# Kernel study: the router's statistics and high parts of all even tiles moved among the heads of a contraction

## The reference, cut to what matters

```python
x = x + _L0_xattn_ref(ctx, ctx, _layernorm(x), ssm_kernel, D, 8)      # long convolution, 32 heads
x = x + _L0_ffn_ref(_layernorm(x), router_w, router_b, expert_w, expert_b)
x = x + _L1_xattn_ref(_layernorm(x), ctx, ctx, Wh, wg_w, wo_w, ...)
x = x + _L1_ffn_ref(_layernorm(x), Wg, Wu, Wd, Wr, Ag, Bg, Au, Bu, Ad, Bd)
...
def _L0_ffn_ref(x, router_w, router_b, expert_w, expert_b):
    logits = xf @ router_w + router_b           # 2048 tokens, 512 features, 16 experts
    S = softmax(logits)
    G, idx = top_k(S.T, 128)                    # each expert picks its 128 best tokens
    out = einsum('ekh,hd->ekd', xf[idx], expert_w) + expert_b
    y = zeros(...).at[idx].add(G[..., None] * out)
```

## Time and profile before

| | |
|---|---|
| median of 3 runs | 1077.47 us (1075.81 to 1080.92) |
| the profiled execution | 1082.89 us |
| its span, first to last instruction | 1080.9 us |
| PE busy | 1045.9 us, 97% of the span |
| DVE, ACT, POOL busy | 580.8, 446.9, 614.0 us |
| last sum of the contraction ends | 188.53 us from the span's start |
| logits complete, softmax starts | 225.31 us |

### The profile page before, as it was taken

One profiled execution on the slowest core, in us unless ns is written; L12 is line 12 of the kernel. 1 busy time (PEld: TensorE's weight loads), 2 busy tenths in 40 slices (PEclk: granted clock), 3 DMA queues, 4 the chain that ended last, 5 costly groups with the idle time before them and its releaser, 6 DMA issues.

```text
span 1080.9 us, 13184 instructions
## 1 busy us (share of the span) xinstructions
PE 1045.9 (97%) x4865; PEld 847.1 (78%) x4865; DVE 580.8 (54%) x1039; ACT 446.9 (41%) x796; POOL 614.0 (57%) x456
## 2 busy tenths in 40 slices
PE   5999998899999999999999999999999999999998
PEld 4777776666689988877788888888888888888886
DVE  6998998848865644784522533325333253342224
ACT  4665444721575547554333322233232233222232
POOL 4888887110224562212367776667766677767662
PEclk9999999889999999999999999999999999999999
DMA  7611210000020020033232222542225332232211
GB/s 242 223 49 62 55 51 20 1 1 1 0 79 1 1 70 1 1 131 138 86 110 74 73 73 73 183 151 98 73 73 170 125 133 76 74 112 93 86 61 39
DMA packets 24543, 85.48 MB, mean 79 GB/s; under 512 B 3152, under 2 KB 4832, under 8 KB 23712
## 3 DMA queue, kind: packets, MB, share of 16 engines
q1 hardware_dynamic: 22432, 81.24, 22.0%
q10 hardware_dynamic: 2048, 3.41, 0.9%
HBM read 74.86 MB, written 9.78 MB: 78 GB/s over the span
## 4 chain that ended last, share of the span: by engine, by line
PE 63%; DVE 1%; POOL 1%; issue 1%; ACT 0%; POOLq 0%
PE banks L318 21%; PE banks L319 20%; PE banks L320 20%; PE banks L313 1%; PE banks L1458 1%; PE banks L1467 0%; POOL wgl L661 0%; DVE stat L1724 0%; POOL gul L687 0%; DVE xres L2112 0%; POOL xtr L644 0%; PE banks L1524 0%; DVE hf L2123 0%; DVE xres L1990 0%; DVE xf L1999 0%
## 5 line engine op out<-in xcount | busy, mean ns | idle before, releaser
L2123 DVE TENSOR_TENSOR hf<-banks,silu 128x512 f32<-128x512 f32 x132 | 91.3, 691 | 323.3 <-PE banks L320 322.1
L687 POOL TENSOR_TENSOR gul<-wst,guh 128x1280 fp32r<-128x1280 f32 x44 | 129.9, 2953 | 142.5 <-DVE guh L2006 135.5
L697 POOL TENSOR_TENSOR hl<-hf,hh 128x512 fp32r<-128x512 f32 x129 | 178.7, 1420 | 8.6 <-ACT hh L1077 8.6
L1113 PE MATMUL banks<-kv,strip 128*128 128x288 f32 x640 | 160.6, 410 | 2.1 <-DVE strip L1656 2.1
L1077 ACT ACTIVATE hh<-hf 128x512 fp32r<-128x512 f32 x132 | 83.6, 633 | 190.3 <-DVE hf L2123 190.3
L1113 PEld LDWEIGHTS banks<-kv,strip 128*128 128x128 f32 x640 | 121.4, 192 | 34.7 <-DVE strip L1656 2.5
L1075 ACT ACTIVATE silu<-banks 128x512 f32<-128x512 f32 x132 | 78.9, 598 | 167.2 <-PE banks L320 167.0
L318 PE MATMUL banks<-xf,guh 128*128 128x512 f32 x352 | 137.2, 390 | 0.9 <-POOL gul L687 0.9
L319 PE MATMUL banks<-xf,guh 128*128 128x512 f32 x352 | 137.0, 389 | 0.0
L320 PE MATMUL banks<-xf,gul 128*128 128x512 f32 x352 | 136.9, 389 | 0.0
L586 POOL TENSOR_TENSOR rstd<-vare,mhalf 128x2 f32<-128x2 f32 x32 | 25.6, 800 | 160.3 <-DVE vare L1737 160.2
(11 more groups left out here) (291 smaller groups left out, 2215.1 us busy)
## 6 DMA issues: line engine op xcount, KB each, us to landing
wst<-in_chunk_w SPq DMA_DIRECT2D x44, 960.0 KB, 4.7
strip<-toep SPq DMA_DIRECT2D x29, 256.0 KB, 3.1
xf_s<-xf SPq DMA_DIRECT2D x2, 2048.0 KB, 6.9
out<-xres SPq DMA_DIRECT2D x16, 256.0 KB, 2.1
xf<-xf_s SPq DMA_DIRECT2D x8, 512.0 KB, 5.8
mk<-hot_s SPq DMA_DIRECT2D x14, 256.0 KB
xres<-in_x ACTq DMA_DIRECT2D x4, 512.0 KB, 7.9
xres<-in_x SPq DMA_DIRECT2D x2, 1024.0 KB, 5.4
```

Source lines behind the costliest of these rows:

```text
L687: pool.tensor_tensor(gul[:, u, :], wst[:, u, 0:GU_W], f(guh[:, u, :]), ALU.subtract).then_inc(gul_ready, 1)
L697: pool.tensor_tensor(hl[:, u, s, :], hf[:, s, :], f(hh[:, u, s, :]), ALU.subtract)\
L1113: mm = pe.matmul(dst, strip[:, h % 3, far:far + P], view(kv, h % 3, m * BATCH * PAIRS, [[PAIRS, BATCH], [1, PAIRS]]), start=m == 0, stop=m ...
L2123: dve.tensor_tensor(hf[:, s, :], banks[:, 7, :], silu[:, s % 2, :], ALU.mult).then_inc(mul_done, 1)
```

## The change

`LOG_ORDER` becomes all even tiles, then all odd tiles. Four pairs instead of two (`CONV_PAIRS`) have their statistics taken among the heads, one tile a head, in heads 23 to 30 instead of 24 to 27; POOL's first two roots stand at heads PAIR_HEAD + 3 and + 5, so they come a head earlier, and the two others behind its last head; pairs 2 and 3 use new small buffers (`slots`). ACT makes `high(0)` to `high(3)` and `apply(2)` ahead of END_CONV. The tail of the router is written anew on PE, ACT and DVE: one pair of odd tiles a turn, `LOW_ACT` gains i = 6, the expert part is taken between pairs 2 and 3, and each group of logits is one block.

```diff
-        LOG_ORDER = (0, 2, 4, 6, 1, 3, 5, 7, 8, 10, 9, 11, 12, 14, 13, 15)
+        LOG_ORDER = tuple(range(0, TILES, 2)) + tuple(range(1, TILES, 2))
-        SUM_HEAD, PAIR_HEAD = HEADS // 2 + 2, HEADS // 2 + 8
-        LOW_ACT = (0, 2, 4, 8, 12)
-        CONV_PAIRS = 2
+        SUM_HEAD, PAIR_HEAD = HEADS // 2 + 2, HEADS // 2 + 7
+        LOW_ACT = (0, 2, 4, 6, 8, 12)
+        CONV_PAIRS = 4
...
+            pair_root(2)
+            pair_root(3)
+            pool.wait_ge(pair_rstd, CONV_PAIRS)
...
+            act.wait_ge(y_free, HEADS - 1)
+            act.wait_ge(pr_pool, HEADS - 1)
+            for i in range(4):
+                high(i)
+            apply(2)
             after(act, END_CONV)
-            for n in range(TILES // 2):
-                if n > 1:
-                    apply(n)
-                if n == 6:
+            low(0)
+            low(2)
+            for n in range(3, TILES // 2):
+                apply(n)
+                if n == 7:
                     logits_out(0)
-                if n > 0:
-                    low(2 * n - 2)
-                high(2 * n)
-                high(2 * n + 1)
+                high(2 * n - 2)
+                high(2 * n - 1)
+                low(2 * n - 2)
+            high(TILES - 2)
+            high(TILES - 1)
...
-            for i in range(4):
-                turn_x(i)
+            turn_x(0)
+            turn_x(1)
+            leave_low(0)
+            turn_x(2)
+            turn_x(3)
+            leave_low(2)
             after(pe, END_CONV)
-            turn_o(4)
-            turn_o(5)
-            leave_low(0)
+            turn_o(8)
+            turn_o(9)
+            turn_x(4)
+            turn_x(5)
             pe.wait_ge(pick_set, 3)
             pe.wait_ge(wB_ready, 2 + KB)
...
+            for n in range(3, TILES // 2):
+                if n < TILES // 2 - 1:
+                    for i in (2 * n + 4, 2 * n + 5):
+                        if i < TILES:
+                            summed(pe, i - 2)
+                            turn_o(i)
+                if n == 3:
+                    expert_parts(KB)
+                leave_low(2 * n - 2)
+                turn_x(2 * n)
+                turn_x(2 * n + 1)
+                if n == 6:
                     low_made(pe, 1)
+                    low_made(pe, 9)
+                    for k in range(KB):
+                        logits(0, k)
                 if n == 7:
+                    low_made(pe, 11)
+                    for k in range(KB):
+                        logits(1, k)
                     by_token(0)
...
-                if PAIR_HEAD <= h < PAIR_HEAD + 4:
+                if PAIR_HEAD <= h < PAIR_HEAD + EVENS:
                     n, j = divmod(h - PAIR_HEAD, 2)
                     pair(n, (j,))
             after(dve, END_CONV)
...
-            low(TILES - 4)
-            low(TILES - 3)
-            low(TILES - 2)
-            low(TILES - 1)
+            low(1)
+            for n in range(CONV_PAIRS, TILES // 2):
+                add_conv(2 * n)
+                add_conv(2 * n + 1)
+                pair(n)
+                for i in ((3,), (5, 7), (9, 10), (11, 13))[n - CONV_PAIRS]:
+                    if n < TILES // 2 - 1:
+                        low(i)
+            low(11)
+            low(13)
+            low(14)
+            low(15)
```

More of the change, by code:

```diff
@@ L142, in build, with slots @@
             ("ebx", [P, DIM], F32R), ("pick", [P, P], F32R), ("minus", [P, P], F32R), ("bitc", [P, 3 * STEPS + 1], I32), ("whf", [P, RHEADS, P], F32))
+        stat62, mom2, vare2, rstd2, nmr2 = place(
+            W_AT + 20480, ("stat62", [P, GROUP, 6], F32), ("mom2", [P, GROUP, 2], F32), ("vare2", [P, 2, GROUP], F32),
+            ("rstd2", [P, GROUP], F32), ("nmr2", [P, GROUP], F32))
+        def slots(n):
+            s = slice(2 * (n % 2), 2 * (n % 2) + 2)
+            if n in (2, 3):
+                return stat62[:, s, :], mom2[:, s, :], vare2[:, :, s], rstd2[:, s], nmr2[:, s]
+            return stat6[:, s, :], mom[:, s, :], vare[:, :, s], rstd[:, s], nmr[:, s]
         ye, = place(XH_AT, ("ye", [P, KB * TOKENS], F32))
@@ L579, in pair_root @@
             def pair_root(n):
-                s = slice(2 * (n % 2), 2 * (n % 2) + 2)
+                _, means, var, roots, negated = slots(n)
                 if n < CONV_PAIRS:
                     pool.wait_ge(pair_stats, 2 * n + 2)
-                    pool.tensor_scalar(vare[:, 0, s], mom[:, s, 1], EPS, None, ALU.add).then_inc(pair_var, 1)
+                    pool.tensor_scalar(var[:, 0, :], means[:, :, 1], EPS, None, ALU.add).then_inc(pair_var, 1)
                 pool.wait_ge(pair_var, n + 1)
-                pool.tensor_tensor(rstd[:, s], vare[:, 0, s], mhalf[:, s], ALU.pow).then_inc(pair_pow, 1)
+                pool.tensor_tensor(roots, var[:, 0, :], mhalf[:, 0:2], ALU.pow).then_inc(pair_pow, 1)
                 pool.wait_ge(pair_pow, n + 1)
                 if n < CONV_PAIRS:
-                    for j in range(s.start, s.stop):
-                        i = pool.tensor_scalar(nmr[:, j:j + 1], mom[:, j, 0:1], rstd[:, j:j + 1], -1.0, ALU.mult, ALU.mult)
+                    for j in range(2):
+                        i = pool.tensor_scalar(negated[:, j:j + 1], means[:, j, 0:1], roots[:, j:j + 1], -1.0,
+                                               ALU.mult, ALU.mult)
                     i.then_inc(pair_rstd, 1)
                 else:
-                    pool.tensor_tensor(nmr[:, s], vare[:, 1, s], rstd[:, s], ALU.mult).then_inc(pair_rstd, 1)
+                    pool.tensor_tensor(negated, var[:, 1, :], roots, ALU.mult).then_inc(pair_rstd, 1)
             root(0)
@@ L628, in low @@
                                    by_eighth(f(cch[:, q % 2, :])), ALU.subtract).then_inc(ccl_ready, 1)
-            for n in range(2, TILES // 2):
+            for n in range(CONV_PAIRS, TILES // 2):
                 pair_root(n)
@@ L773, in apply @@
                     rows = ret if 2 * TILES <= i < 3 * TILES else xres
-                    act.activation(xn[:, j, :], rows[:, tile_of(i), :], ACT.Identity,
-                                   bias=nmr[:, j:j + 1], scale=rstd[:, j:j + 1]).then_inc(xn_ready, 1)
+                    _, _, _, roots, negated = slots(n)
+                    act.activation(xn[:, i % GROUP, :], rows[:, tile_of(i), :], ACT.Identity,
+                                   bias=negated[:, i % 2:i % 2 + 1], scale=roots[:, i % 2:i % 2 + 1]).then_inc(xn_ready, 1)
             for i in range(4):
@@ L1710, in pair @@
             def pair(n, part=range(2)):
-                s = 2 * (n % 2)
-                if n >= 2:
+                stats_of, means, var, _, _ = slots(n)
+                if n == 2:
+                    dve.wait_ge(wB_ready, 1 + KB)
+                if n in (CONV_PAIRS, CONV_PAIRS + 1):
+                    dve.wait_ge(pair_rstd, CONV_PAIRS)
+                    dve.wait_ge(xn_ready, 2 * n - 6)
+                elif n > CONV_PAIRS:
                     dve.wait_ge(xn_ready, 2 * n - 2)
@@ L1723, in pair @@
                     tile = LOG_ORDER[2 * n + j] if n < TILES // 2 else (2 * n + j) % TILES
-                    i = dve.bn_stats(stat6[:, s + j, :], rows[:, tile, :])
+                    i = dve.bn_stats(stats_of[:, j, :], rows[:, tile, :])
                 if 1 not in part:
@@ L1729, in pair @@
                 for j in range(2):
-                    i = dve.bn_aggr(mom[:, s + j, :], stat6[:, s + j, :])
+                    i = dve.bn_aggr(means[:, j, :], stats_of[:, j, :])
                 i.then_inc(pair_stats, 1)
@@ L1758, in _ @@
             after(dve, END_CONV)
-            for n in range(1, TILES // 2):
-                if n > 1:
-                    pair(n)
-                if n in (1, 2, 4, 6):
-                    for i in SUM_ORDER[TILES // 2 + (0, 2, 4, 6)[(1, 2, 4, 6).index(n)]:][:2]:
-                        add_conv(i)
-                if n > 1:
-                    low(2 * n - 4)
-                    low(2 * n - 3)
-            low(TILES - 4)
-            low(TILES - 3)
-            low(TILES - 2)
-            low(TILES - 1)
+            low(1)
+            for n in range(CONV_PAIRS, TILES // 2):
+                add_conv(2 * n)
[8 more added lines that the diff above has]
+            low(15)
             n_vec = [0]
```

29 lines of the change are left out of this document (5 added, 24 removed).

## The result

The changed kernel took 1081.6 us (median of 7 runs, 1080.8 to 1084.0), the kernel before, run beside it, 1076.4 (1075.4 to 1080.9). The ratio is 1.0045, 95% interval 1.003 to 1.0059: 4.8 us slower, under the 0.5% at which I put a difference that can be told, and 4.4 was forecast. The two profiled executions don't show it in their spans: 1080.9 us before, 1080.2 changed.

The account below looks back on a forecast made before the run. PE, busy 97% of the span, bounds the kernel, so the seam only shifts what follows. Terms 0.8 + 0.1 + 1.0 + 1.4 = 3.3, plus 1.1 for the clock: 1077.47 + 4.4 = 1081.9 us, range 1077 to 1087.

Parts of the forecast that it names:

- Contraction's end, +0.8: Heads 23 to 30: POOL's roots delay sums and heads 28 to 30 lose catch-up room; last sum ends 0.8 us later.
- the roots' hits: POOL's pair roots, 1.59 us each, at heads 26 and 28 make DVE's sums of heads 27 and 29 wait.
- To the last pair, +0.1: Contraction's end to last pair: 3.5 us of pairs and 2 us of high parts removed return as waits; 20.0 against 19.9.
- Both stalls: Between contraction's end and last pair: ACT stands 4.1 us at low(4), DVE idles 2.6 us ahead of low(10).
- high(12), +1.0: Router tail: ACT makes high(12) only after logits_out(0), so turn_x(15) comes 6.8 behind the last pair's start instead of 5.9.
- logits(1) as one block, +1.4: Router tail on PE: all four blocks of logits(1) follow the last turn instead of one; six more matmuls of 0.24.
- The clock, +1.1 taken from 0 to 2.3: PE's wait from 210.7 to 214.8 may drop its clock to half, making the tail late; total +3.3 if it stays, +5.6 if not.
- The point between: Total of +4.4 us, chosen between +3.3 (PE's clock stays full) and +5.6 (it falls).
- Slower by over 0.5%, the clock decides: Rival, PE between 203 and 220: half clock costs middle 1 and tail 2.3, total +6.6, 1084; chance 0.35.
- The other losses: Middle of the seam: turns at half clock lengthen each round of turn, high, low by 0.4, so the middle loses 1.
- The stalls do not bind: Rival: ACT not held at low(4), DVE not at low(10); softmax -3.1 us, 1074.4; 0.15 with the third rival.
- the third rival: Nothing moves: the search's half-clock stretch starts elsewhere, returning 2 to 3 us; +2, 1079.5; 0.15 with the stalls rival.

Follow-up runs that it names:

- the last kernel: Changed kernel with all winning edits together (pairs a head earlier, expert part, low(10) and logits_out(0) later, high(12) earlier), against the kernel before: ratios 0.9996 and 0.9986.

## Why the prediction was right

**The time.** 1081.9 forecast, 1081.6 measured. That these two agree within 0.3 us is partly luck: the forecast added 4.4 to a median of three runs (1077.47), and with seven the kernel before has 1076.42, which is 5.2 below the changed one. What can be compared is the sum of +4.4 against +4.9 in the seam (two profiles of each) and +4.8 by the ratio.

**Contraction's end, +0.8.** Measured +0.85 (D1, both pairs of profiles). The waits stand where they were forecast, at the sums of heads 27 and 29. I named two causes together, the roots' hits and the bn_stats behind them. The run with the pairs a head earlier has the same hits and D1 as before: the hits cost nothing that lasts once head 30 is free of bn_stats, and with bn_stats there DVE has no room to catch up. Putting the roots a head later only moved the hit. No run has bn_stats at head 30 without the hits, so whether it would cost anything alone stays open.

**To the last pair, +0.1.** Measured 19.72 and 19.40, against 19.87 and 19.12 before: -0.15 by the first pair of profiles, +0.28 by the second, both within what two profiles of one kernel differ by. Both stalls are where the text put them: ACT 3.86 us at low(4) (forecast 4.1), DVE 2.52 at low(10) (2.6). That they, and not the work, set this stretch is shown: either one taken away brought the last pair 2.9 us nearer, both together (with the pairs a head earlier) 5.2 to 6.0.

**high(12), +1.0, and logits(1) as one block, +1.4.** With the clock held, the run with matmuls in the gap has logits(1) 7.10 behind the last pair instead of 6.25, +0.85, and from there to the softmax 12.03 instead of 10.66, +1.37. Both terms hold within 0.2, by this one profile.

**The clock, +1.1 taken from 0 to 2.3.** This was the mis-sized term of the sum: 2.15 in the first profile (21.28 against 19.13), 1.26 in the second (20.39 against the same 19.13), on average 1.7. The point between was a guess between ends. It rested on a reading that does not hold: the text says that rows show the clock at both levels "after waits of this length", that is some 4 us, but the waits ahead of its two rows were shorter, 2.36 and 1.31 us ahead of 189 and 1.01 ahead of 211:

```profile
186.20 1.06 PE L1165 MATMUL banks<-cst,xn 128*128 128x128 f32 x8 [2.36 <-DVE pr L1697]
...
210.97 0.63 PE L1165 MATMUL banks<-cst,xn 128*128 128x128 f32 x4 [1.01 <-DVE xtl L1743]
```

So the full clock at 211 was no evidence that the clock would stay through 3.9. In the four profiles with the gap as in the changed kernel (2.34 us in the second one, 3.9 in the three others) it fell to half every time, in the gap or right behind it. The text also took 4 us as the longest half-clock stretch; it was 6.8 us in the first profile, of which 1.2 lay in the gap.

By the Trainium skill (TensorE: Matmul & The Clock Gate, section The HAM clock gate) the throttled state is the default one and idle time brings it back, and by that rule alone the sum was +5.6. The window at 209, idle and granted 0.66, agrees with it, and the first profile's seam (+5.07) lies between the two sums.

**The rivals.** "Slower by over 0.5%, the clock decides" was close: the clock fell in its place, between 203 and 220, at a price of 1.3 to 2.2 us where it needed 2.1. The other losses it needed (turns at half clock in the middle) did not come in the first profile, and the two ratios, 1.0045 and 1.0051, lie on both sides of its 0.5%. "The stalls do not bind" is refuted by the two edits that took them away. The search was 1.8 us shorter in one profile of the changed kernel and as long as before in the other: the third rival's effect exists, but two executions of one kernel differ by it, so it is not shown to come from the change.

## What to carry to other kernels

When work is taken off two engines that hand tiles to each other in program order, first look for the instruction in each that stands behind a third engine's long block: here 5.5 us of work removed were given back to within 0.3 us by two such places, and moving one block (the expert part) took back some 3.4 of the 4.8 us lost. A filler belongs where its engine would otherwise stand and nothing that follows is ready yet, not merely "somewhere early" or in front of the last step that others wait for: the same block cost 2.9 us ahead of leave_low(4) and gained 1.3 to 2.2 in the gap ahead of leave_low(12). And a gap on PE can be priced twice: once by its length if it is on the path, once by what runs at half clock behind it, here 1.3 to 2.2 us.

## What was not expected of the hardware

The granted clock is no function of the program alone. The same kernel kept 1.00 from 190 to 220 in one execution and fell to 0.50 at 202.3 in another, in the middle of back-to-back matmuls, some 1 to 3 us behind short gaps (1.06 us, at 200.8). The stretches lasted from 3.4 to 10.2 us, and eleven of fourteen profiles had one between 200 and 217; whether it cost anything hung on what lay under it. 3.4 us of it, mostly under logits(0), left D3 at 19.13 in the run with matmuls in the gap, and the run with the expert part late has 19.12 without any; in the changed kernel, 6.8 us in the gap and under the last turns and logits(1) made it 21.28. What puts the stretch at one place or the other in executions of one program stays open; so does why the times of the last kernel show only 0.4 to 1.5 us of the 2.1 that its seams gained. The search and the part behind the gate vary by as much between executions, but the fourteen profiles are too few to say whether this kernel's do so to its loss.
